# A gated FFN on one core: earlier products, signs from ACT, and two sets of PSUM banks in the down stage

## What is computed

```python
x = x + ffn(cond(x, ids, W, b))            # x: 32 x 128 x 512, 64 weight matrices of 512 x 512

cond:  einsum('bsd,bdh->bsh', x, W[ids]) + b[ids][:, None, :]

ffn:   x    = act_qdq(x)                   # one scale for the whole tensor: its max over 32767
       up   = act_qdq(x @ dq(w_up).T)      # 512 -> 1536, dq: 4 bit blocks of 32
       gate = act_qdq(x @ dq(w_gate).T)
       sig  = fixed_qdq_u16(sigmoid(gate))
       gate = act_qdq(gate * sig)
       o    = act_qdq(gate * up)
       return o @ dq(w_down).T             # 1536 -> 512
```

## Time and profile of the kernel before

| | us |
|---|---|
| median of 3 runs (1015.52 to 1016.12) | 1015.73 |
| the profiled execution, its own time | 1016.78 |
| its span, first to last instruction | 1015.0 |
| PE busy | 903.1 (89%) |
| DVE busy | 673.1 (66%) |
| ACT busy | 406.0 (40%) |
| DMA, mean | 254 GB/s |

### The profile page before, as it was taken

The page is one execution under the profiler, slowest core; times in us unless marked ns, Lnnn a source line. Parts: engine busy times, 40 slices in busy tenths (PEclk is TensorE's granted clock), DMA queues, the critical chain, the costliest instruction groups (busy, mean ns, idle before and its releaser), DMA issues. The chain is left out here.

```text
span 1015.0 us, 13534 instructions
## 1 busy us (share of the span) xinstructions
PE 903.1 (89%) x4904; PEld 487.4 (48%) x4904; DVE 673.1 (66%) x739; ACT 406.0 (40%) x442; POOL 4.0 (0%) x17
## 2 busy tenths in 40 slices
PE   6999998999999999999999999930049799999998
PEld 6999993444444444444444444410014344444443
DVE  0356779645656453487787879669979498677740
ACT  1113331433334333588777883229822122112100
POOL 0000000000000000000000000000000000000000
PEclk9999999999999999999999999975569899999999
DMA  8998863223352222799999865999985699777611
GB/s 284 376 382 292 304 216 152 107 112 124 124 218 94 94 93 102 267 333 381 357 369 359 313 234 202 406 421 383 400 321 208 257 353 322 283 277 257 248 62 62
DMA packets 69206, 257.52 MB, mean 254 GB/s; under 512 B 6130, under 2 KB 6130, under 8 KB 69170
## 3 DMA queue, kind: packets, MB, share of 16 engines
q1 hardware_dynamic: 59794, 206.59, 55.5%
q10 hardware_dynamic: 9376, 50.48, 12.2%
HBM read 180.23 MB, written 76.81 MB: 253 GB/s over the span
## 5 line engine op out<-in xcount | busy, mean ns | idle before, releaser
L479 ACT ACTIVATE stage<-bank 128x512 f32<-128x512 f32 x192 | 111.6, 594 | 211.4 <-PE bank L654 174.7
L686 PE MATMUL bank<-wt_down,o_even 128*128 128x512 f16 x192 | 73.7, 384 | 80.5 <-DVE o_even L1082 80.5
L652 PE MATMUL bank<-xq_head,wt_gate 128*128 (+1 forms) x336 | 128.1, 381 | 4.3 <-DVE xq_head L856 4.3
L654 PE MATMUL bank<-xq_head,wt_gate 128*128 (+1 forms) x336 | 128.1, 381 | 0.0
L653 PE MATMUL bank<-xq_head,wt_gate 128*128 (+1 forms) x336 | 127.9, 381 | 0.0
L652 PE MATMUL bank<-xq_head,wt_up 128*128 x336 | 127.3, 379 | 0.0
L653 PE MATMUL bank<-xq_head,wt_up 128*128 x336 | 127.3, 379 | 0.0
L654 PE MATMUL bank<-xq_head,wt_up 128*128 x336 | 127.3, 379 | 0.0
L869 DVE TENSOR_REDUCE tile_max<-stage 128x1 f32<-128x1536 f32 (+1 forms) x62 | 108.4, 1749 | 25.4 <-ACT stage L479 25.3
L602 PE MATMUL bank<-xt,w_ring 128*128 128x128 f32 x1024 | 121.3, 277 | 2.2 <-ACT xt L432 2.2
L571 ACT ACTIVATE ucode<-up_again,scal 128x1536 int16<-128x1536 f32 x32 | 50.5, 1577 | 180.7 <-DVE up_again L1058 180.7
(11 more groups left out here) (123 smaller groups left out, 1310.5 us busy)
## 6 DMA issues: line engine op xcount, KB each, us to landing
w_ring<-in_L_cond_W_dram SPq DMA_DIRECT2D x32, 1024.0 KB, 7.3
gate_scratch<-stage ACTq DMA_DIRECT2D x32, 768.0 KB, 3.3
gate_ring<-gate_scratch SPq DMA_DIRECT2D x32, 768.0 KB, 7.1
up_scratch<-stage ACTq DMA_DIRECT2D x32, 768.0 KB, 6.8
up_again<-up_scratch SPq DMA_DIRECT2D x32, 768.0 KB, 4.3
gate_again<-gate_scratch SPq DMA_DIRECT2D x32, 768.0 KB, 5.9
up_ring<-up_scratch SPq DMA_DIRECT2D x30, 768.0 KB, 9.7
product_scratch<-prod_ring SPq DMA_DIRECT2D x23, 768.0 KB, 5.5
```

The lines of the kernel that those rows point to most:

```text
L479: nc.scalar.activation(stage[:, q % 2, n % PIECE_TILES, :], psum[n % BANKS][:, :], ACT.Copy)\
L652: nc.tensor.matmul(bank[:, :], w_hi, x_hi, start=(k == 0), stop=False)
L654: mm = nc.tensor.matmul(bank[:, :], w_lo, x_hi, start=False, stop=(k == KH - 1))
L686: nc.tensor.matmul(psum[r][:, :], o_hi, wt_down[:, 0, k, :], start=(k == 0), stop=False)
```

## The change

- `SPILLED` falls from 23 to 19, so 13 products stay on chip. The last four (j of 28 and over) are written into the `gate_ring` slot of their own gate piece, beside 4 in `prod_ring` and 5 in `prod_kept`. `back_ring` is filled from slot 4 on; two reloads are issued at the end of pass 1, and reload k from 2 on waits for code step k + 8.
- `PASS1` becomes 6, 5, 6, 5, 6, 6 (cut off at 32 steps, which is in the third quarter of chunk 5). `PASS2` starts in that quarter and ends in the third quarter of chunk 7. The code steps of a quarter now stand ahead of its `piece_max`.
- In the down stage ACT makes the sign of gate as an int16 (`sgn`, new activation `Sign`) and then the code of up, straight into `ocode`. DVE multiplies the two (`signed_up`, now an int16 `tensor_tensor`), and the product with the activation code is made in place. The code of up for piece n waits until the low part of piece n - 2 is done. The `ucode` buffer is gone.
- All chunks of the down stage are multiplied piece by piece. Even chunks use `psum[0]` to `psum[3]`, odd chunks use `psum[4]`, `psum[5]` and the banks of `wt_bank` and `bias_bank`. The results of chunk i are finished while the codes of chunk i + 2 are made, instead of those of chunk i + 1. `piece_used` frees a slot of product codes piece by piece.

```diff
-PASS1 = (5, 5, 5, 5, 6, 6)
-LEAD = 4
+PASS1 = (6, 5, 6, 5, 6, 6, 0, 0)
+LEAD = 8
-SPILLED = 23
+SPILLED = 19
-PASS2 = ((0, 0, 0, 3), (4, 4, 4, 4), (4, 4, 4, 1))
+PASS2 = {5: (0, 0, 2, 5), 6: (5, 4, 4, 4), 7: (4, 3, 1, 0)}
...
+            if j >= PIECES - RING:
+                return gate_ring[:, j % RING, :]
...
+        def down_bank(h, r):
+
+            if h == 0:
+                return psum[r][:, :]
+            if r < 2:
+                return psum[BPC + r][:, :]
+            if r == 2:
+                return wt_bank[:, :, :, :].rearrange("p h k n -> p (h k n)").bitcast(f32)
+            return bias_bank[:, :]
...
-                if k < RING:
-                    sp.wait_ge(code_made, PIECES - RING + k + 1)
-                elif k < AHEAD:
-                    sp.wait_ge(sigq_made, PIECES - AHEAD + k + 1)
+                if k < AHEAD - RING:
+                    sp.wait_ge(sigq_made, PIECES - AHEAD + RING + k + 1)
                 else:
                     sp.wait_ge(act_made, KEPT + k - AHEAD + 1)
...
-                    act.wait_ge(sign_made, Q * i + q + 1)
+                    act.wait_ge(gate_again_in[q % 2], 32 * i + (16 if q < 2 else 32))
                     if not first or q >= 2:
-                        act.wait_ge(prod_used, Q * i + q - 1)
-                    nc.scalar.activation(ucode[:, q % 2, :], up_again[:, q % 2, :], ACT.Copy, scale=k_u)\
+                        act.wait_ge(signed_made, Q * i + q - 1)
+                    nc.scalar.activation(sgn[:, q % 2, :], gate_again[:, q % 2, :], ACT.Sign).then_inc(sgn_made, 1)
+                    act.wait_ge(up_again_in[q % 2], 32 * i + (16 if q < 2 else 32))
+                    if not first or q >= 2:
+                        act.wait_ge(o_ready, Q * i + q - 1)
+                    nc.scalar.activation(ocode[:, q % 2, :], up_again[:, q % 2, :], ACT.Copy, scale=k_u)\
                         .then_inc(ucode_made, 1)
...
+            def down_quarter(i, h, q, first):
+                pe.wait_ge(o_ready, Q * i + q + 1)
                 for r in range(BPC):
+                    if q == 0 and not first:
+                        pe.wait_ge(y_made, BPC * (i - 2) + r + 1)
+                    bank = down_bank(h, r)
+                    for t in range(PIECE_TILES):
...
-                V.scalar_tensor_tensor(out=up_again[:, q % 2, :].bitcast(i32), in0=gate_again[:, q % 2, :].bitcast(i32),
-                                       scalar=-2 ** 31, in1=up_again[:, q % 2, :].bitcast(i32),
-                                       op0=ALU.bitwise_and, op1=ALU.bitwise_xor).then_inc(sign_made, 1)
+                dve.wait_ge(ucode_made, Q * i + q + 1)
+                dve.wait_ge(sgn_made, Q * i + q + 1)
+                V.tensor_tensor(ocode[:, q % 2, :], ocode[:, q % 2, :], sgn[:, q % 2, :], ALU.mult).then_inc(signed_made, 1)
...
                     for q in range(Q):
                         product_codes(i, q, h, False, last and h == 1)
-                        finish_tile(i - 1, q, False)
+                        finish_tile(i - 2, q, h, first and h == 0)
```

More of the change, by code:

```diff
@@ L377, in _ @@
                 sp.wait_ge(ucode_made, n + 1)
+                sp.wait_ge(sgn_made, n + 1)
+                load_again(n + 2, n)
+            for n in range(Q + 1, 2 * Q + 1):
+                sp.wait_ge(ucode_made, n + 1)
+                sp.wait_ge(sgn_made, n + 1)
                 load_again(n + 2, n)
@@ L681, in _ @@
                 tile_matmul(2 * CHUNKS - 1, CHUNKS - 1, n, wt_up, False)
[L684 to L688, removed]
@@ L690, in down_chunk @@
-            def down_chunk(i, h):
-                for r in range(BPC):
[L692 to L705, removed]
+            def down_quarter(i, h, q, first):
+                pe.wait_ge(o_ready, Q * i + q + 1)
+                for r in range(BPC):
+                    if q == 0 and not first:
+                        pe.wait_ge(y_made, BPC * (i - 2) + r + 1)
+                    bank = down_bank(h, r)
+                    for t in range(PIECE_TILES):
+                        k = PIECE_TILES * q + t
+                        o_hi, o_lo = (o_slot(h, q)[:, part, t, r * P:(r + 1) * P] for part in range(2))
+                        nc.tensor.matmul(bank, o_hi, wt_down[:, 0, k, :], start=(k == 0), stop=False)
+                        nc.tensor.matmul(bank, o_hi, wt_down[:, 1, k, :], start=False, stop=False)
+                        mm = nc.tensor.matmul(bank, o_lo, wt_down[:, 0, k, :], start=False, stop=(k == NT - 1))
@@ L706, in _ @@
                     if q == Q - 1:
                         mm.then_inc(out_done, 1)
-            down_chunk(1, 1)
+                if q < Q - 1:
+                    mm.then_inc(piece_used, 1)
+            pe.wait_ge(tile_copied, 2 * NT * CHUNKS)
+            for h in range(2):
+                for q in range(Q):
+                    down_quarter(h, h, q, True)
             with pe.Fori(1, CHUNKS // 2) as pair:
                 for h in range(2):
-                    down_chunk(2 * pair + h, h)
+                    for q in range(Q):
+                        down_quarter(2 * pair + h, h, q, False)
@@ L1072, in product_codes @@
                     signed_up(i + (q + 1) // Q, (q + 1) % Q)
-                dve.wait_ge(ucode_made, n + 1)
-                V.scalar_tensor_tensor(out=ocode[:, q % 2, :], in0=act_piece(n), scalar=k_o, in1=ucode[:, q % 2, :],
+                dve.wait_ge(signed_made, n + 1)
+                V.scalar_tensor_tensor(out=ocode[:, q % 2, :], in0=act_piece(n), scalar=k_o, in1=ocode[:, q % 2, :],
                                        op0=ALU.mult, op1=ALU.mult).then_inc(prod_used, 1)
                 dve.wait_ge(prod_used, n + 1)
-                if not first and q == 0:
+                if not first and q < Q - 1:
+                    dve.wait_ge(piece_used, (Q - 1) * (i - 2) + q + 1)
+                elif not first:
                     dve.wait_ge(out_done, BPC * (i - 1))
@@ L1091, in finish_tile, with down_pair @@
                     dve.wait_ge(y_out_done[r % 2], 32 * i + (0 if r < 2 else 16))
-                V.scalar_tensor_tensor(out=y_out[:, r % 2, :], in0=psum[r][:, :], scalar=k_y, in1=x_res[:, r % 2, :],
+                V.scalar_tensor_tensor(out=y_out[:, r % 2, :], in0=down_bank(h, r), scalar=k_y, in1=x_res[:, r % 2, :],
                                        op0=ALU.mult, op1=ALU.add).then_inc(y_made, 1)
[L1095 to L1103, removed]
+            for h in range(2):
+                for q in range(Q):
+                    product_codes(h, q, h, True)
+            def down_pair(pair, first, last):
                 for h in range(2):
```

77 lines of the change are left out of this document (38 added, 39 removed).

## The result

The median after is 1002.30 us (four runs, 1001.08 to 1003.47), beside 1015.92 for the kernel before. The prediction was 1000.3 with a range from 995.5 to 1008.5. The profiled execution took 1002.87 us and its span is 1000.9, so it is to be compared with 1016.78 and 1015.0 before.

The account below looks back on a forecast made before the run. Bounds taken: PE in the up stage, then DVE waiting for reloads, DMA in stage 4, PE with two holes in the down stage. -7.4 + 1.7 - 10.8 + 1 = -15.5 from 1016.78 gives 1001.3 profiled, median 1000.3, range 995.5 to 1008.5.

Parts of the forecast that it names:

- earlier landing: End of stage 4: first gate piece of the down stage lands at 735.0 instead of 742.38, term -7.4 us.
- Pass 1, 7.4 us: Pass 1: product steps take 5.7 us, so the last product starts at 607.5, 7.4 us earlier.
- Pass 2 moves by the same amount: Pass 2: the last code step also moves by 7.4 us, to 670.2, with 17 reloads outstanding in both kernels.
- the floor that the prediction named: Scale that opens stage 4: it cannot come before 672.2, set by PE's own end of the up stage.
- fewer spills alone bring nothing: Pass 2: four fewer spills do not shorten it, being paid by two reloads fetched ahead instead of six.
- Stage 4 ends with the last reload and not with the scale: Stage 4: up pieces queue behind the last reload, so its end moves 7.4 us earlier, to about 732.3.
- Opening, 1.7 us more: Down stage opening: landing to first matmul takes 8.8 us instead of 7.1, with sign and code both on ACT.
- Holes, 10.8 us: Down stage: PE's holes of 7.07 and 1.65 us go, with 2.06 us of lower clock; 10.8 us gained.
- A new stall of 1 us at the bank of row 3: Down stage: DVE finishes row 3 of chunk 0 at 71.5 us, PE wants the bank at 70.2; 1 us, once.
- DMA as the bound of pass 1: Rival for pass 1: DMA can't hold 377 GB/s, the 7.4 us are lost, time 1007.8; chance 0.15.
- PE's banks running full: Rival for pass 1: ACT falls behind until PE's six banks fill; slower than before, 1027 at 320 GB/s; chance 0.04.

Follow-up runs that it names:

- e7: Kernel after, but in odd product steps DVE makes the magnitude before it waits for the sigmoid; 996.51 us, ratio 0.9796 to the kernel before.
- e5: Kernel after with 23 spilled products again (9 kept) at the new step tables, up pieces prefetched two steps later; 1007.17 us, ratio 0.9907.
- e8: Kernel after with the magnitude ahead of the sigmoid wait in odd product steps and the signs made on DVE; 996.33 us, ratio 0.9791.
- e4: Kernel after with the step tables of the kernel before, 13 products still kept; 1007.47 us, ratio 0.9911.
- e9: Kernel after, with the piece maximum ahead of the code steps in the first three quarters of the last up chunk; 1001.17 us, ratio 0.9838.
- e1: Kernel before with only the down stage changed: piece by piece over two sets of four banks; 1006.52 us, ratio 0.9897.
- e2: Kernel before with only the new step tables, 19 spilled products and their slots, down stage untouched; 1011.74 us, ratio 0.9946.
- e6: Kernel after with the signs made on DVE as before and ACT's code in its own buffer; 999.89 us, ratio 0.9841.
- e11: Second run of the kernel after with the signs made on DVE, beside the unchanged kernel after; 1000.76 us, ratio 0.9833.

## Why the prediction was right, point by point

Most of the mechanisms stood; the one that ends stage 4 did not. In the profiled execution 15.5 us were forecast and 13.9 measured. The terms were -7.4 (earlier landing), +1.7 (opening), -10.8 (holes) and +1 (stall), and in the spans they measured -5.1, +1.6, -10.7 and 0. The landing missed by 2.3 us, and the stall that did not come hid 1 of them, which was luck. By its own steps:

- **Pass 1, 7.4 us.** Measured 5.9. The pace of 5.7 a step was 5.74 (1.2 us over 31 steps), and the first product started 0.24 later. Neither is more than executions differ by: P is 177.1 to 178.1 in five profiles with these tables, and 179.1 and 179.6 in two. The 5.7 was taken from chunks of before and not from a cause. What sets the pace is ACT's waits for the magnitude, as e7 shows: the prediction said that ACT and DVE would run free, and they still waited for each other.
- **Pass 2 moves by the same amount.** Right as far as it goes: from last product to landing it is 127.3 to 128.4 in all profiles but those of e5, e7 and e8, at a pace of 5.94 and of 5.7 alike. At 5.44 (e7 and e8) it is 132.5, since PE's own end then holds the scale, the floor that the prediction named. The claim that fewer spills alone bring nothing is borne out by e4 to 0.2 us. What it left out is that the new tables without the kept products lose most of their gain (e5).
- **Stage 4 ends with the last reload and not with the scale.** Wrong, though the pace inside it was right (1.88 us a piece, as before). The last code step came 6.5 us earlier, the scale 4.9, and the landing 5.1: it followed the scale, as in all thirteen profiles (e9 above). The prediction had the scale itself nearly right, 5.7 us earlier, with the second maximum in front of it (4.4 us from last code step to scale before, 6.05 after), and held that the end would not feel it. Of the 2.3 us that the landing missed, 1.5 are the last product; the other 0.8 are 1.65 for that second maximum, less 0.6 by which the last code step came sooner behind the last product, less 0.2 from scale to landing.
- **Opening, 1.7 us more.** Measured 1.63. Each term came within some 0.2 us of its row. No table load came in: the groups of the kernel after show two of them, one at its start (L454) and one at the first Sigmoid (L546), and none at Sign. The kernel before has the same two (L432 and L524), so the prediction's one load in the trace was a misreading: the earlier trace rows covers the up stage alone.
- **Holes, 10.8 us.** Right: 10.7 in the profile, 10.3 in the medians of e1. What held the fourth piece back was misread (e1 above), and the change removes that too.
- **A new stall of 1 us at the bank of row 3.** Wrong: there is none. A piece takes 5.98 us in the chain instead of 6.2: the handovers take 0.13 where 0.2 was put, and the multiply and the product behind it overlap by 0.08. The second piece was ready 8.3 and not 8.7 after PE's start. The bank was free at 814.8, 1.9 us before PE asked for it.
- **Rivals.** DMA as the bound of pass 1: not so, 404 GB/s in e7 and a step faster than 5.7. The Trainium skill, page "DMA: Bandwidth & Descriptors", section "Where 436 GB/s comes from", puts the limit for one core between HBM and SBUF at about 358 GB/s; the windows of pass 1 here show 368 to 404 with reads and writes mixed, and the measurement decides. PE's banks running full: PE idle nowhere in the up stage, and not in e7 either.

## What to carry to other kernels

A second set of accumulators, with the reloads issued early enough to use it, is worth a try where the engine that empties them has other work in the same queue: it turns a deadline of one row into one of a whole chunk. Here the two came together, for 10.7 us. The order of the matmuls by itself only made new waits. Work taken off DVE where it was not the bound brought nothing here, and as one more link in a serial opening it cost 1.3 us. To find what opens a stage, take the distance from each candidate to its end over several variants: the one that stays the same (here the scale, 60 us) is the cause to look into first. And where two engines hand pieces to each other, look at the waits of under 2 us that repeat each step: fifteen of up to 1.6 us, on an operation that needed nothing of what it was queued behind, cost more than all that the signs could have brought.

## What the runs showed beyond expectation

DMA at a share of 1.00 in the windows was not yet the bound: it moved 368 GB/s at 1.00 in the kernel after and 404 at 1.01 in e7, and in neither was a gate load waited for from 420 to 600 us. And in the kernels that have the new passes and the signs on DVE (e2, e6, e8, e11) the opening takes 7.43 and not 7.08 us: DVE starts the first product 0.46 us behind the end of ACT's code (739.03 after 737.00 + 1.57 in e6) instead of 0.1. The cause stays open: the operations of the scale were done by 737.91 in e6, so it is not they.
